# Cross-attention with a quantized feed-forward on one core: edge products of token blocks 1 to 3 in one run of 32 six-column products

## What is computed

```python
h = bit_linear(x, w1)                    # 256 -> 1024, x rounded to 8 bits per token, w1 to -1, 0, 1
h = depthwise_conv1d(h.transpose(0, 2, 1), conv_w, conv_b)   # 3 taps along the tokens, padding 1
h = jax.nn.silu(h.transpose(0, 2, 1))
return bit_linear(h, w2)                 # 1024 -> 256, h rounded to 8 bits per token
x = x + ffn(layernorm(x))
```

## Time and profile before

| | |
|---|---|
| three runs | 437.04, 437.31 and 438.87 us, median 437.31 us |
| the profiled execution | 437.79 us, of it 435.6 us span |
| PE busy | 409.6 us (94%) |
| DVE busy | 376.7 us (86%) |
| ACT busy | 313.8 us (72%) |
| POOL busy | 85.2 us (20%) |

### The profile page before, as it was taken

One profiled execution on the slowest core, in us unless ns is written; L12 is line 12 of the kernel. 1 busy time (PEld: TensorE's weight loads), 2 busy tenths in 40 slices (PEclk: granted clock), 3 DMA queues, 4 the chain that ended last, 5 costly groups with the idle time before them and its releaser, 6 DMA issues.

```text
span 435.6 us, 13927 instructions
## 1 busy us (share of the span) xinstructions
PE 409.6 (94%) x5967; PEld 279.1 (64%) x5967; DVE 376.7 (86%) x598; ACT 313.8 (72%) x368; POOL 85.2 (20%) x115
## 2 busy tenths in 40 slices
PE   6999997799999999999999999999999978899985
PEld 5666674567667666666666766666676744566673
DVE  5789987987896889789889879879879899999994
ACT  2476687579979756756756766766667589999984
POOL 2356544920000130020130020120011010121200
PEclk9999999999999999999999999999999998999999
DMA  7702000612111111111111201111111000001002
GB/s 232 212 1 73 2 0 13 219 52 66 48 38 63 51 38 51 51 39 62 51 39 38 75 29 48 64 38 51 39 39 39 2 0 2 2 25 50 26 26 78
DMA packets 26516, 22.52 MB, mean 52 GB/s; under 512 B 6152, under 2 KB 26196, under 8 KB 26452
## 3 DMA queue, kind: packets, MB, share of 16 engines
q1 hardware_dynamic: 26112, 21.59, 15.4%
q10 hardware_dynamic: 340, 0.01, 0.0%
HBM read 6.91 MB, written 2.10 MB: 21 GB/s over the span
## 4 chain that ended last, share of the span: by engine, by line
PE 57%; DVE 25%; ACT 12%; issue 3%; DMA 2%; DVEq 0%; ACTq 0%; POOL 0%; SPq 0%
PE sc L1708 14%; DVE arena L726 13%; PE heads L1725 6%; PE heads L1726 5%; PE heads L1727 5%; PE heads L1533 4%; ACT arena L1296 3%; PE sc L1545 3%; ACT qq L1385 3%; PE by L1613 2%; ACT qq L1393 2%; PE bx L1545 2%; PE by L1545 2%; PE sc L1812 2%; DMA kst<-kk 1%
## 5 line engine op out<-in xcount | busy, mean ns | idle before, releaser
L726 DVE SCALAR_TENSOR_TENSOR arena<-arena 128x1024 bf16<-128x1024 f32 x160 | 193.8, 1242 | 30.9 <-ACT arena L1296 29.9
L1296 ACT ACTIVATE arena<-sc,kb 128x1024 f32<-128x1024 f32 x160 | 169.7, 1114 | 68.3 <-PE sc L1708 68.1
L1725 PEld LDWEIGHTS heads<-v,arena 128*128 128x128 bf16 x1280 | 117.0, 97 | 39.2 <-issue 28.3
L1725 PE MATMUL heads<-v,arena 128*128 128x65 f16 x1280 | 130.2, 194 | 3.8 <-DVE arena L726 3.5
L1726 PE MATMUL heads<-v,arena 128*128 128x64 f16 x1280 | 129.3, 195 | 0.0
L1727 PE MATMUL heads<-v,arena 128*128 128x65 f16 x1280 | 128.7, 192 | 0.0
L1708 PE MATMUL sc<-qs,kst 64*128 64x512 f16 x960 | 118.0, 378 | 2.6 <-DVE kk L668 1.5
L1726 PEld LDWEIGHTS heads<-v,arena 128*128 128x128 bf16 x1280 | 118.7, 97 | 0.1
L1727 PEld LDWEIGHTS heads<-v,arena 128*128 128x128 bf16 x1280 | 118.7, 99 | 0.0
L1708 PEld LDWEIGHTS sc<-qs,kst 64*128 64x128 f16 x960 | 40.0, 94 | 48.6 <-issue 5.0
L523 POOL TENSOR_SCALAR frs<-fmv 128x2 f32<-128x2 f32 x8 | 7.9, 991 | 150.9 <-DVE fmv L794 150.9
(11 more groups left out here) (220 smaller groups left out, 595.9 us busy)
## 6 DMA issues: line engine op xcount, KB each, us to landing
kst<-kk SPq DMA_DIRECT2D x80, 128.0 KB, 2.0
xs<-in_x SPq DMA_DIRECT2D x8, 256.0 KB, 5.0
qs<-qq SPq DMA_DIRECT2D x16, 128.0 KB, 2.1
out<-cbuf SPq DMA_DIRECT2D x7, 256.0 KB, 2.1
xs<-in_ctx SPq DMA_DIRECT2D x6, 256.0 KB, 5.9
xs<-in_L_ffn_w SPq DMA_DIRECT2D x1, 1024.0 KB, 7.3
cbuf<-in_L_ffn_w SPq DMA_DIRECT2D x1, 1024.0 KB, 9.5
arena<-in_L_xattn_W_kv SPq DMA_DIRECT2D x2, 256.0 KB, 4.2
```

Of the source, the lines that this page charges most:

```text
L726: e.scalar_tensor_tensor(out=rest[:, j, :, :], in0=prob[:, j, :, :], scalar=SHRINK, in1=probh[:, j, :, :], op0=ALU.mult, op1=ALU.subtract) ...
L1296: a_.activation(prob[:, j, :, :], sc[(j + 1) % 2][:, :, :], ACT.Exp, bias=kb[:, bass.ds(i * QUAD + j, 1)]).then_inc(exp_done[j], 1)
L1725: t_.matmul(o, hi, row[:, 0:OW], start=first and sub == 0, stop=False, skip_group_check=True)
```

## The change

The blocks 1 to 3 get their edge products together. A matmul of the new run has six columns, the two edge columns of each of the three blocks, by the same weights. The run stands once, in the first pass of the loop behind `hidden(1, 3)`, and it waits until all rows are in `xd` (`xd_ready` at 8). VectorE multiplies 48 numbers once in place of 16 numbers three times. Block 0 keeps its own run, and `edges` grows to hold all four blocks.

```diff
-        edges = sb("edges", [P, J, 2], F32)
+        edges = sb("edges", [P, J, NF, 2], F32)
...
+        def edge_columns(k, w, first):
+            at_ = xd[:, k, w, 0:1] if first else xd[:, k, w, FB:FB + 1]
+            return bass.AP(at_.tensor, at_.offset, [at_.ap[0], (FB, 1 if first else NF - 1), (FB + 1, 2)])
...
+            def edge_products(first):
+                ns = slice(0, 1) if first else slice(1, NF)
+                count_ = 1 if first else NF - 1
+                dve.wait_ge(s["edge_ps"], 1 if first else 2)
+                taps = cw[:, :, 0:3:2].rearrange("p j (n e) -> p j n e", n=1).to_broadcast([P, J, count_, 2])
+                e.tensor_tensor(edges[:, :, ns, :], edge_bank(first), taps, ALU.mult).then_inc(s["edge_step"], 1)
...
             def edge_taps(n, k):
-                dve.wait_ge(s["edge_step"], n + 1)
+                dve.wait_ge(s["edge_step"], 1 if n == 0 else 2)
...
-            def hidden_edges(n):
-                pe.wait_ge(s["xd_ready"], min(NB, 2 * n + 3) if n else NB - 2)
-                if n == 1:
+            def hidden_edges(first):
+                pe.wait_ge(s["xd_ready"], NB - 2 if first else NB)
+                if not first:
                     pe.wait_ge(s["x1_ready"], NB)
-                elif n > 1:
-                    pe.wait_ge(s["uf_ready"], (n - 1) * FT)
...
             def tokens_first(n, t):
-                if t == 1 and n < NF - 1:
-                    pe.wait_ge(s["edge_step"], n + 2)
+                if m == 1:
+                    pe.wait_ge(s["edge_step"], 2)
...
                 hidden(1, 2)
-                hidden_edges(1)
                 late_rows_first(1)
                 for n in range(1, NF):
                     tokens_first(n - 1, 0)
                     hidden_ahead(n, 3)
                     if n > 1:
                         hidden_first(n - 2, 3)
-                    if n > 1:
-                        hidden_edges(n)
+                    if n == 1:
+                        hidden_edges(False)
                     hidden_ahead(n, 4)
```

More of the change, by code:

```diff
@@ L267, in xattn_ffn, with edge_bank @@
         ob = [bank[7][:, 0:D], bank[6][:, 0:D]]
-        def edge_bank(n):
-            b = bank[7][:, D:D + 2 * J] if n == 0 else bank[5][:, 0:2 * J]
-            return b.rearrange("p (j e) -> p j e", e=2)
+        def edge_bank(first):
+            if first:
+                return bank[7][:, D:D + 2 * J].rearrange("p (j n e) -> p j n e", n=1, e=2)
+            return bank[5][:, 0:2 * J * (NF - 1)].rearrange("p (j n e) -> p j n e", n=NF - 1, e=2)
+        def edge_columns(k, w, first):
+            at_ = xd[:, k, w, 0:1] if first else xd[:, k, w, FB:FB + 1]
+            return bass.AP(at_.tensor, at_.offset, [at_.ap[0], (FB, 1 if first else NF - 1), (FB + 1, 2)])
         def product_bank(n, t):
@@ L924, in right_tap @@
                                        op0=ALU.mult, op1=ALU.add).then_inc(s["taps_done"], 1)
-            def edge_products(n):
-                dve.wait_ge(s["edge_ps"], n + 1)
-                e.tensor_tensor(edges[:, :, :], edge_bank(n), cw[:, :, 0:3:2], ALU.mult).then_inc(s["edge_step"], 1)
+            def edge_products(first):
[4 more added lines that the diff above has]
+                e.tensor_tensor(edges[:, :, ns, :], edge_bank(first), taps, ALU.mult).then_inc(s["edge_step"], 1)
             def edge_taps(n, k):
                 js = slice(2 * k, 2 * k + 2)
-                dve.wait_ge(s["edge_step"], n + 1)
+                dve.wait_ge(s["edge_step"], 1 if n == 0 else 2)
                 dve.wait_ge(s["taps_done"], n * J + 2 * k + 2)
                 c = ct[n % 3][:, js, 0:FB:FB - 1]
-                e.tensor_tensor(c, c, edges[:, js, :], ALU.add).then_inc(s["edge_done"], 1)
+                e.tensor_tensor(c, c, edges[:, js, n, :], ALU.add).then_inc(s["edge_done"], 1)
             def largest(n, t):
@@ L1003, in feed_forward @@
                 heads_weighed(NCH * HP - 1, NCH - 1, HP - 1)
-                edge_products(0)
+                edge_products(True)
                 left_tap(0, 1)
@@ L1050, in feed_forward @@
                     largest(n - 1, 0)
-                    edge_products(n)
+                    if n == 1:
+                        edge_products(False)
                     left_tap(n, 2)
@@ L1833, in hidden_edges @@
                         for w in range(2):
-                            last = t_.matmul(edge_bank(n)[:, j, :], w1t[:, k, j * P:(j + 1) * P], xd[:, k, w, n * FB:n * FB + FB + 2:FB + 1],
+                            last = t_.matmul(edge_bank(first)[:, j, :, :], w1t[:, k, j * P:(j + 1) * P], edge_columns(k, w, first),
                                              start=(q == 0), stop=(q == 3))
@@ L1903, in feed_forward @@
                 hidden(0, 2)
-                hidden_edges(0)
+                hidden_edges(True)
                 hidden(0, 3)
```

## The result

The changed kernel has a median of 439.89 us over 12 runs (438.53 to 441.71), the kernel before one of 437.13 us over its 12 runs beside them (436.04 to 438.87). The ratio is 1.0056, with a 95% interval of 1.0037 to 1.0075: the change makes the kernel slower, by 2.4 us (1.6 to 3.3). The forecast was 437.6 us with a range up to 438.6 us, so the result lies outside it.

A forecast was written before the change was run, and what follows sets the result against it. ScalarE was taken to lead the first half of each pass, TensorE the second. +0.37 us (moved run) and -0.10 us (two removed runs) gave +0.27 us on the 437.31 us median: 437.6 us, range 436.7 to 438.6 us.

The forecast's parts named there:

- What bounds the kernel: In the passes from quantize(0, 0) on, ScalarE leads in the first half of each pass and TensorE in the second.
- the two runs that go: Edge runs of blocks 2 and 3: 1.7 us of TensorE time removed, worth only -0.10 us, 0.05 us each.
- The expected wait of 1.1 us for `quantize`: TensorE near 389 and 407 us: its 0.22 us wait for ScalarE grows to about 1.1 us.
- Price of the run: New run on TensorE: 32 six-column matmuls cost 26.6 ns each, 0.85 us, like two columns; upper price 0.95 us more.
- The 0.1 us to spare at VectorE: New run's last result is there near 369.2 us; VectorE asks for it at 369.29 us, just in time.
- The moved run: Block 1's run goes behind hidden(1, 3), delaying hidden(1, 4), center(1, 4) and quantize(0, 0): +0.37 us.
- Steps 1 to 6: Turn to block 1: successive start times from late_rows_first(1) through the new run to quantize(0, 0), which comes 0.37 us later.
- the sum's last one: Whole execution: +0.27 us in the span, with 2.19 us around it, put on the 437.31 us median: 437.6 us.
- may also be fetched otherwise, which the trace doesn't price: Instruction streams, within the rival of nothing measurable or a code shift: shorter streams may be fetched otherwise, unpriced; rival's chance 0.16.
- The clock rival: TensorE's added idle time before 389.63 and 407.60 us lets its clock fall: some 2 us per fall, 439.6 us; chance 0.07.

The follow-up runs named there:

- the padded kernels: Never-executed matmuls appended behind the kernel before or the changed kernel; changed kernel with 64: 437.66 us, 128: 438.83 us, 192: 437.33 us, 32: 438.38 us.
- the kernel that had its 2 us inside the span: Against the changed kernel, the two unexecuted feed-forward copies hold separate edge products, the executed copy stays merged: 439.79 us, ratio 1.0050 to the kernel before.

## Why the prediction was wrong

**What bounds the kernel, and the two runs that go: right.** From `quantize(0, 0)` to the last VectorE instruction the profiles have 61.30 us before and 61.20 us after, -0.10 us as forecast, out of 1.7 us of TensorE time. The expected wait of 1.1 us for `quantize` did not come in that form. There are 0.21 us for `whole` in front of `tokens_first(1, 1)`, which I had not listed, and 0.41 us in front of `hidden_first(1, 0)`; the rest of the freed time is spread in gaps too short for a bracket. This has no effect on the sum.

**Price of the run: right.** 366.78 to 367.63 us, 0.85 us for 32 matmuls of six columns. This is 26.6 ns each, as with two columns. The Trainium skill, "TensorE: Matmul & The Clock Gate", section "LDWEIGHTS (loading the stationary operand)", gives some 107 ns for a load of 128 columns; as the spacing the trace does not bear this out. The 32 cycles for four parallel chunks stand in the Trainium skill, in the same page's section "Weight-path perf modes — Fast Weight Load (FWL) and DoubleRow", as the theory for fp8 weights, beside a measured gain of about 2x. The weights here are f16, and no run shows whether the load sets the 26.6 ns. The product of 48 numbers takes up 0.13 us (367.81 to 367.94 us) for the 0.12 us expected. The 0.1 us to spare at VectorE was not there: from `largest(0, 0)` to the product it is 1.27 us (366.54 to 367.81 us) in place of 1.13 us, and the product starts 0.03 us behind the end of the run, so it waited some 0.14 us, too little for a bracket.

**The moved run: mechanism right, size too small.** Steps 1 to 6 came in their order. Taken from the start of `silu(0, 3)`, `tokens_first(0, 0)` begins 1.20 us later (1.12 expected), `hidden(1, 4)` 3.82 us (3.72) and `quantize(0, 0)` 5.57 us (5.43). The term was +0.37 us and measured +0.51 us. The 0.14 us lie in the handover from `silu` to `tokens_first` and in groups that take 0.90 us behind a wait where I had put 0.87 us. The span thus costs 0.4 us by the traces in place of 0.27 us. The other profiles bear this out: from the edge product of block 0 to the last VectorE instruction it takes 84.61 to 84.63 us in three profiles with the order of before, and 85.04 to 85.16 us in five with the merged run. Where the clock fell late the difference is gone: 85.99 us in the order of before, 85.90 and 86.00 us merged.

**The step that failed is the sum's last one.** I took the time around the span for a constant, 2.19 us, and put the in-span sum on the median. It was 3.4 to 3.7 us in the changed kernel. The sentence on shorter streams that "may also be fetched otherwise, which the trace doesn't price" named the place, but had no price and no end in the range. It is worth 1.2 to 1.6 us here, some three times the whole effect of the schedule. That it goes with the length of code that is not executed, and not with executed work, is shown by the padded kernels; by what mechanism, stays open. Where the tail is short the change takes 437.66, 437.33 and 438.38 us, close to the forecast of 437.6 us, but that is in part luck: the part outside is 1.85 us there, 0.3 us less than in the kernel before, which hides most of the 0.4 us in the span, and the kernels before beside them had 438.15 and 437.74 us and not 437.31 us. Against these no difference is seen (ratios 0.9991 to 1.0006).

**The clock rival: did not come.** The clock did not fall in the passes where TensorE got idle time. It falls once near the turn, from 358 to 367 us, in eleven of the fourteen profiles, in both orders of work, and not at all there in the other three; it costs up to 1.4 us or nothing by where it lands.

## What to carry to other kernels

Work saved on the busiest engine is worth what that engine's wait behind it allows, here 0.1 us out of 1.7 us; and a run that is merged must stand where its engine was idle, not in front of the product that the next engine waits for. When a change alters the length of a program with branches, compare time less span as well as the span: if it moved, append code that is never executed and measure again before judging the schedule.

## What the hardware showed unexpectedly

- 32 never executed matmuls, 64 instructions, behind an otherwise unchanged program took the median time outside the span from 3.4 or 3.7 us down to 1.85 us; 128 matmuls brought 3.22 us back, and 192 took it to 1.86 us.
- The time outside the span repeats within some 0.15 us in the kernels with a short tail (2.10 to 2.24 us in 35 runs), while it scatters from 2.52 to 4.23 us in the changed kernel. A scattering rest is itself a sign, but a steady one proves nothing: the kernel that had its 2 us inside the span showed 1.59 to 1.68 us outside.
- The same order of instructions took 23.3 or 24.7 us on one piece of 23 us, by where a fall of TensorE's clock to 1.2 GHz came to lie.
